# Last stage of a GNN + LSTM kernel: scale and shift of z2 moved into TensorE's products

## The reference

```
agg = A_hat @ x1                                  # per graph
h   = relu(batchnorm(agg @ W1.T + b1, g1, be1))   # 256 features
z2  = h @ W2.T + b2                               # 128 features
y   = (z2 - mean(z2)) * rsqrt(var(z2) + eps) * g2 + be2   # mean, var over all 16384 rows
out = layernorm(x1 + y)                           # over the 128 features of each row
```

## Time and profile before

| | us |
|---|---|
| median of 3 runs | 802.19 (801.57 to 805.52) |
| profiled execution, its own time | 802.61 |
| its span, first to last instruction | 800.8 |
| TensorE busy | 775.7 (97%) |
| VectorE busy | 716.3 (89%) |
| ScalarE busy | 596.7 (75%) |
| GpSimd busy | 107.7 (13%) |
| mean granted TensorE clock | 0.994 |

### The profile page before, as it was taken

One profiled execution on the slowest core, in us unless ns is written; L12 is line 12 of the kernel. 1 busy time (PEld: TensorE's weight loads), 2 busy tenths in 40 slices (PEclk: granted clock), 3 DMA queues, 4 the chain that ended last, 5 costly groups with the idle time before them and its releaser, 6 DMA issues.

```text
span 800.8 us, 15544 instructions
## 1 busy us (share of the span) xinstructions
PE 775.7 (97%) x4964; PEld 532.6 (67%) x4964; DVE 716.3 (89%) x1826; ACT 596.7 (75%) x1186; POOL 107.7 (13%) x117
## 2 busy tenths in 40 slices
PE   8999999999999999999999999999999989999995
PEld 6666777777767777777677767767776656444542
DVE  4787989999999999999999999999999988788996
ACT  4876777777777777777777778686868765697598
POOL 0000000000000000000000000000000101187695
PEclk9999999999999999999999999999999999999998
DMA  5010001010101010101010101010000000155245
GB/s 202 29 51 1 1 28 54 27 53 28 53 28 54 26 52 26 52 26 52 26 52 26 52 26 52 27 52 28 27 27 28 27 27 27 52 168 174 84 180 210
DMA packets 17694, 44.45 MB, mean 56 GB/s; under 512 B 2032, under 2 KB 3184, under 8 KB 17520
## 3 DMA queue, kind: packets, MB, share of 16 engines
q1 hardware_dynamic: 17504, 43.81, 15.2%
q10 hardware_dynamic: 144, 0.07, 0.0%
HBM read 27.09 MB, written 16.78 MB: 55 GB/s over the span
## 4 chain that ended last, share of the span: by engine, by line
PE 81%; DVE 9%; ACT 5%; issue 2%; DMA 1%; POOL 0%; ACTq 0%; DVEq 0%; POOLq 0%
PE gate_bank L964 15%; PE gate_bank L965 14%; PE gate_bank L979 6%; PE gate_bank L989 6%; PE gate_bank L1038 5%; PE front_bank L874 3%; PE back_bank L918 3%; ACT z L1187 3%; PE front_bank L879 3%; PE front_bank L891 3%; PE front_bank L885 3%; PE gate_bank L948 3%; PE gate_bank L949 3%; PE gate_bank L950 3%; PE gate_bank L972 3%
## 5 line engine op out<-in xcount | busy, mean ns | idle before, releaser
L964 PE MATMUL gate_bank<-h_hi,w_hi 128*128 128x256 f16 (+2 forms) x528 | 162.6, 308 | 4.4 <-DVE h_lo L1404 2.9
L965 PE MATMUL gate_bank<-h_hi,w_lo 128*128 128x256 f16 (+2 forms) x528 | 162.5, 308 | 0.0
L1126 ACT ACTIVATE gate_i<-gate_bank,lstm_bias 128x512 f32<-128x512 f32 (+2 forms) x176 | 99.5, 566 | 61.9 <-PE gate_bank L989 32.1
L1126 ACT ACTIVATE gate_o<-gate_bank,lstm_bias 128x512 f32<-128x512 f32 (+2 forms) x176 | 100.0, 568 | 31.2 <-PE gate_bank L989 20.8
L979 PE MATMUL gate_bank<-h_lo,w_hi 128*128 128x256 f16 (+2 forms) x384 | 116.1, 302 | 0.0
L964 PE MATMUL gate_bank<-s_hi,w_hi 128*128 128x256 f16 (+2 forms) x384 | 112.7, 302 | 0.6 <-DVE s_hi L1401 0.4
L1387 DVE SCALAR_TENSOR_TENSOR gate_f<-gate_o,gate_f 128x512 f32<-128x512 f32 (+2 forms) x176 | 94.7, 538 | 20.4 <-ACT gate_f L1132 19.4
L965 PE MATMUL gate_bank<-s_hi,w_lo 128*128 128x256 f16 (+2 forms) x384 | 112.6, 301 | 0.0
L765 POOL TENSOR_TENSOR rstd<-veps,neg_half 128x8 f32<-128x8 f32 x15 | 26.3, 1751 | 628.0 <-DVE veps L1326 628.0
L1132 ACT ACTIVATE gate_f<-cell 128x512 f32<-128x512 f32 (+2 forms) x176 | 89.7, 510 | 28.0 <-DVE cell L1384 14.7
L1126 ACT ACTIVATE gate_g<-gate_bank,lstm_bias 128x512 f32<-128x512 f32 (+2 forms) x176 | 99.5, 565 | 0.8 <-PE gate_bank L972 0.2
(11 more groups left out here) (261 smaller groups left out, 1722.2 us busy)
## 6 DMA issues: line engine op xcount, KB each, us to landing
x_kept<-normed_sb SPq DMA_DIRECT2D x16, 512.0 KB, 2.6
z<-x_kept SPq DMA_DIRECT2D x16, 512.0 KB, 3.7
rows_sb<-in_x SPq DMA_DIRECT2D x15, 512.0 KB, 3.3
x_front<-in_x SPq DMA_DIRECT2D x15, 512.0 KB, 4.5
out<-z SPq DMA_DIRECT2D x15, 512.0 KB, 3.1
z<-in_wr SPq DMA_DIRECT2D x1, 1536.0 KB, 7.0
x_front<-in_x SPq DMA_DIRECT2D x2, 256.0 KB, 3.7
out<-z SPq DMA_DIRECT2D x2, 256.0 KB, 2.6
```

What stands on the lines that cost most here:

```text
L964: mm(dst, w[0], v[0], start=start, stop=False)
L965: mm(dst, w[1], v[0], start=False, stop=False)
L1126: ins = activation(acts[gate][h][:, 0:n], gate_bank[h][bank_of(job, gate)][:, 0:n], ACT.Tanh if gate == "g" else ACT.Sigmoid, bias=lstm_bi ...
```

## The change

The step 1 above goes away, with its staging tile and `y_scaled`. The scale and the shift become two 128x128 tiles, `scale_diag` and `shift_diag`: the identity times the scale, and times the shift, made once by VectorE when the two are known. A third tile holds ones. All three lie in h0T. For each block of 128 columns TensorE now takes an ordinary fp32 product of z2 (stationary) with `scale_diag` (moving), which transposes and scales, and another of ones (stationary) with `shift_diag` (moving), which puts the shift into every row (`shift_in`). `x1_rows` is issued first, as the product that starts the bank. VectorE makes the ones at the start of the z2 stage, ahead of the splitting of W2. TensorE's loop over t is written out, with constant addresses.

```diff
@@ -477,7 +477,8 @@
         normed = normed_sb
-        scaled = [mixed, h0T, x_front, rows_sb]
+        scale_diag, shift_diag, ones = (h0T[:, 0, n * P:(n + 1) * P] for n in range(3))
         shapes = (("bn", (GB, 6)), ("comb", (3, GB)), ("veps", (GB,)), ("rstd", (GB,)), ("mean_rstd", (GB,)))
         terms = {name: [sb(name, [P, *shape])[:]] for name, shape in shapes}
...
@@ -637,20 +638,11 @@
         r_parts = [t[:].bitcast(F16) for t in (x_front, mixed, rows_sb)]
         z2_bank = [gate_bank[0][0], gate_bank[1][0], gate_bank[0][2], gate_bank[1][2]]
         LAST = HALVES // 4 - 1
-        free_at_start = [z2_kept, y_full, y_norm]
+        free_at_start = [z2_kept, y_norm]
         FIRST_LOADS, LOADS = 4, 8
         STAY_WARM = 20
         WARM_UP = 8
         block = ctx.enter_context(nc.Block())
-        def scale_z2(eng, n, t, u):
-            eng.wait_ge(y_full[u], 2 * t + 1)
-            eng.tensor_scalar(scaled[u][:, n, :],
-                              z[:, bass.ds(8 * t + (2 * u + n), 1), 0, :].rearrange("p o n -> p (o n)"),
-                              small[:, 1:2], small[:, 2:3], ALU.mult, ALU.add).then_inc(y_scaled[n][u], 1)
         def flat(t):
             return t.rearrange("p a n -> p (a n)")
...
@@ -788,9 +780,6 @@
                                                 parts[:, j, 0:BANK], ALU.subtract).then_inc(r_split, 1)
             pool.wait_ge(sem_bn2, 2)
             nc.gpsimd.tensor_tensor(small[:, 13:14], small[:, 12:13], neg_half[:, 0:1], ALU.pow).then_inc(sem_bn2_pow, 1)
-            pool.wait_ge(sem_bn2, 3)
-            for u in range(4):
-                scale_z2(pool, 1, 0, u)
             def row_powers(t, u, at=slice(0, GB), seen=0):
...
@@ -802,18 +791,12 @@
                 nc.gpsimd.tensor_tensor(mean_rstd[u][:, at], comb[u][:, 2, at], rstd[u][:, at], ALU.mult
                                         ).then_inc(y_shift[u], 1)
-            for u in range(4):
-                if u == 0:
-                    row_powers(0, 0, slice(0, 4))
-                    row_powers(0, 0, slice(4, 8), 1)
-                else:
-                    row_powers(0, u)
-                scale_z2(pool, 1, 1, u)
+            row_powers(0, 0, slice(0, 4))
+            row_powers(0, 0, slice(4, 8), 1)
+            for u in range(1, 4):
+                row_powers(0, u)
             for t in range(1, LAST + 1):
                 for u in range(4):
-                    if t < LAST:
-                        pool.wait_ge(y_mom[u], 4 * (t + 1 + (u == 0)))
-                        scale_z2(pool, 1, t + 1, u)
                     row_powers(t, u)
...
@@ -1049,21 +1032,28 @@
                           z[:, bass.ds(8 * t + (2 * u + n), 1), 1, :].rearrange("p o n -> p (o n)"),
                           start=first, stop=not first, skip_group_check=True)
+            def shift_in(to, stop=False):
+                for b in range(4):
+                    last = mm(to[:, b * P:(b + 1) * P], ones, shift_diag, start=False, stop=stop and b == 3,
+                              skip_group_check=True)
+                return last
+            def z2_rows(t, u, n, b, stop):
+                at = slice(b * P, (b + 1) * P)
+                return mm(row_bank[u][n][:, at],
+                          z[:, 8 * t + 2 * u + n, 0, at], scale_diag,
+                          start=False, stop=stop, skip_group_check=True)
             def rows_out(t, u, x1_there=()):
                 pe.wait_ge(y_norm[u], t + 1)
                 for n in range(2):
-                    to = row_bank[u][n]
-                    pe.wait_ge(y_scaled[n][u], t + 1)
+                    if n not in x1_there:
+                        x1_rows(t, u, n, True)
+                    shift_in(row_bank[u][n])
                     for b in range(4):
-                        at = slice(b * P, (b + 1) * P)
-                        if n in x1_there:
-                            last = mm(to[:, at], scaled[u][:, n, at], ident[:], start=False, stop=(b == 3),
-                                      skip_group_check=True)
-                        else:
-                            mm(to[:, at], scaled[u][:, n, at], ident[:],
-                               start=(b == 0), stop=False, is_transpose=True, skip_group_check=True)
-                    if n not in x1_there:
-                        last = x1_rows(t, u, n, False)
+                        last = z2_rows(t, u, n, b, b == 3)
                     last.then_inc(y_full[u], 1)
...
@@ -1074,10 +1064,20 @@
                 x1_rows(0, u, n, True)
             for m in range(2, 4):
                 pe.wait_ge(z2_kept[m], CHUNKS // 4 + 1)
-            for u in range(4):
-                rows_out(0, u, ((0, 1), (0,), (), ())[u])
+            pe.wait_ge(z2_terms, 2)
+            for b in range(4):
+                z2_rows(0, 0, 0, b, False)
+            pe.wait_ge(z2_terms, 3)
+            for n in range(2):
+                if n:
+                    for b in range(4):
+                        z2_rows(0, 0, n, b, False)
+                shift_in(row_bank[0][n], True).then_inc(y_full[0], 1)
+            rows_out(0, 1, (0,))
+            for u in range(2, 4):
+                rows_out(0, u)
             pe.wait_ge(x1_back_end, 32)
-            with pe.Fori(1, HALVES // 4) as t:
+            for t in range(1, HALVES // 4):
                 for u in range(4):
                     rows_out(t, u)
...
@@ -1180,24 +1180,17 @@
             with act.Fori(1, CHUNKS // TURN) as c:
                 relus(c)
-            def normed_rows(t, u, sets=range(2)):
-                for n in sets:
-                    for b in range(4):
-                        at = z[:, bass.ds(8 * t + (2 * u + n), 1), 1, b * P:(b + 1) * P]
-                        ins = activation(at.rearrange("p o n -> p (o n)"), row_bank[u][n][:, b * P:(b + 1) * P],
-                                         ACT.Identity, bias=mean_rstd[u][:, 4 * n + b:4 * n + b + 1],
-                                         scale=rstd[u][:, 4 * n + b:4 * n + b + 1])
+            def normed_rows(t, u, first=0, count=GB):
+                for k in range(first, first + count):
+                    n, b = k // 4, k % 4
+                    at = z[:, bass.ds(8 * t + (2 * u + n), 1), 1, b * P:(b + 1) * P]
+                    ins = activation(at.rearrange("p o n -> p (o n)"), row_bank[u][n][:, b * P:(b + 1) * P],
+                                     ACT.Identity, bias=mean_rstd[u][:, k:k + 1], scale=rstd[u][:, k:k + 1])
                 return ins
-            act.wait_ge(sem_bn2, 3)
-            for t, u in ((0, 1), (0, 2), (0, 3), (1, 0)):
-                act.wait_ge(y_full[u], 2 * t + 1)
-                activation(scaled[u][:, 0, :], z[:, 8 * t + 2 * u, 0, :], ACT.Identity, bias=small[:, 2:3],
-                           scale=small[:, 1:2]).then_inc(y_scaled[0][u], 1)
             for n in range(2):
                 act.wait_ge(y_shift[0], n + 1)
-                ins = normed_rows(0, 0, (n,))
+                ins = normed_rows(0, 0, 4 * n, 4)
             ins.then_inc(y_norm[0], 1)
             for u in range(1, 4):
                 act.wait_ge(y_shift[u], 1)
...
@@ -1463,6 +1456,7 @@
             last.then_inc(sem_bn1, 1)
+            ve.memset(ones, 1.0).then_inc(z2_terms, 1)
             ve.tensor_scalar(gw2_sb[:], gw2_sb[:], W_SCALE, None, ALU.mult).then_inc(w2_ready, 1)
             dve.wait_ge(w2_ready, 1)
             ve.tensor_copy(w2_hi, gw2_sb[:]).then_inc(w2_ready, 1)
...
@@ -1544,31 +1538,32 @@
                 return ve.scalar_tensor_tensor(out=veps_t, in0=m2, scalar=1.0 / P, in1=veps_t, op0=ALU.mult,
                                                op1=ALU.add)
-            def row_terms(t, u, scaled_next, sets=range(2), seen=0):
+            def row_terms(t, u, sets=range(2), seen=0, between=()):
                 first_twice = 1 if u == 0 and not seen and not (isinstance(t, int) and t == 0) else 0
                 at = slice(4 * sets[0], 4 * sets[-1] + 4)
                 for n in sets:
-                    dve.wait_ge(y_full[u], 2 * t + n + 2)
+                    dve.wait_ge(y_full[u], 2 * t + n + 1)
                     last = row_stats(row_bank[u][n], bn[u], n)
                 last.then_inc(y_mom[u], 1)
                 for step in range(3):
                     dve.wait_ge(y_mom[u], 4 * (t + first_twice + seen) + step + 1)
                     row_steps(bn[u][:, at, :], comb[u][:, :, at], veps[u][:, at], step).then_inc(y_mom[u], 1)
-                    if step == 1 and scaled_next:
-                        scale_z2(dve, 0, *scaled_next)
+                    if between:
+                        between[step]()
             dve.wait_ge(sem_bn2, 3)
-            scale_z2(dve, 0, 0, 0)
-            row_terms(0, 0, None, (0,))
-            row_terms(0, 0, None, (1,), 1)
+            for k, to in enumerate((scale_diag, shift_diag)):
+                ve.tensor_scalar(to, ident[:], small[:, 1 + k:2 + k], None, ALU.mult).then_inc(z2_terms, 1)
+            row_terms(0, 0, (0,))
```

(11 more changed lines are left out.)

## The result

The changed kernel takes 838.8 us (median of 4 runs, 837.5 to 839.51) against 802.24 before: a ratio of 1.0451, 95% interval 1.0439 to 1.0464. It was run again beside the later experiments and gave 838.05 us, 1.0449 (1.0435 to 1.0463). The profiled execution took 838.18 us with a span of 836.4, so 1.8 us lie around the span as before. The prediction was 839.8, with a span of 838.0.

What follows compares the result with a forecast made beforehand. TensorE, with next to no slack in the last stage, was taken as the bound: start 746.10 + ones 0.2 + products 82.5 + last record 0.16 + tail 9.0 = 838.0 us span, 1.8 around it, 839.8 us; range 835.5 to 845.

Steps and rivals of the forecast that it cites:

- The pitch: Last stage, TensorE: each added full fp32 product of 128 columns takes 0.225 us, 256 of them 57.6 us.
- The ones: Start of the z2 stage: VectorE's memset ahead of splitting W2 delays TensorE by 0.2 us, bounds 0 and 0.3.
- The two tiles, and the first product: Last stage's start: scale's tile takes VectorE 0.34 us, TensorE starts 0.14 later; shift's tile is hidden by the first products.
- No waits on the other engines: Last stage: the others need near half of TensorE's 5.3 us step, so TensorE runs without a gap.
- The 4.9 us of waiting: Last stage before: TensorE's waiting and restarting within 45.3 us, already contained in the subtraction; relieving other engines gives nothing beyond.
- The tail: After TensorE's last product: the same chain to the end as before, 9.0 us; stores possibly 0.7 sooner, not counted.
- B: Last stage: weight loads and products take turns, 0.30 us a record, 154 us in place of 57.6; 936 us, chance 0.02.
- C: Last stage: new products cost 0.11 us each like a transpose, 28.2 us in all; 810.4 us, chance 0.02.
- D: TensorE's steady set: added products fit into what the bound leaves, not slower, down to about 800 us; chance 0.02.
- E: Written-out loop over t: straight code starves TensorE, 0.3 us a set, adding 7 us; 847 us, chance 0.04.

Runs made afterwards that it cites:

- the runs with the dead scalings: Changed kernel with the old 512-column scalings still made on VectorE and GpSimd into unread tiles: 840.85 us; without those of the last turn, 838.4 us.
- the run with the shift's products alone: Kernel before, engines still scaling z2, but the shift comes from 128 products of ones with its diagonal: 825.89 us.
- the wide product with a quarter of the loads: Changed kernel with each set's shift as one fp32 product of 512 columns in place of four of 128: 836.98 us.
- the addition: Changed kernel, but VectorE and GpSimd add the shift to x1 in SBUF before its product: 817.76 us; with GpSimd's addition under VectorE's statistics, 812.39 us.

## Why the prediction was right

The step and its mechanism were as forecast: 839.8 us against a median of 838.8, and against 838.18 for the profiled execution, whose terms follow, in us:

| term | predicted | measured |
|---|---|---|
| VectorE begins the scale's tile | 745.62 + 0.2 | 745.25 |
| from there to TensorE's first product | 0.48 | 0.44 |
| first to last product | 82.66 | 827.99 − 745.69 = 82.30 |
| tail | 9.0 | 836.4 − 827.99 = 8.4 |
| span | 838.0 | 836.4 |

The terms are off by 0.6, 0.04, 0.4 and 0.6 us, all in the same direction, so no error hid another. The two largest lie outside TensorE's stage.

**The pitch** was read from L1060's products, which stood in the kernel before only because three sets had x1 ahead of time. Taken at 0.225, measured 0.223 to 0.224: 0.4 us of the sum.

**The ones** were priced at 0.2 us on TensorE's path and cost 0.01 there. Around them, after:

```profile
690.28 0.34 DVE L1453 SCALAR_TENSOR_TENSOR small<-small,v_sb 128x1 f32<-128x1 f32 x2
690.60 0.17 DVE L1459 MEMSET h0T<- 128x128 f32 x1
690.68 0.23 DVE L1460 TENSOR_SCALAR gw_sb<-gw_sb 128x256 f32<-128x256 f32 x1
```

The next operation begins 0.08 us after the memset, but VectorE does pay: counted from the start of the operation ahead (690.66 before, 690.28 after), the splitting ends after 1.32 us before and 1.42 after. TensorE's first product of the z2 stage comes 1.56 and 1.57 us after the same point, because it had something else ahead of it, 20 warm-up products, here before:

```profile
687.90 4.48 PE L837 MATMUL gate_bank<-s_hi 128*128 128x512 f16 x20
```

They take 20 × 0.216 us, to 692.22, exactly where that first product starts, and after the change from 687.53 to 691.85, the same. VectorE's result was there 0.24 us ahead of it before and is 0.15 us ahead now. So the prediction's reading, that TensorE waits for VectorE's result here, was wrong: there was at least 0.1 us of slack, and the memset fell into it. The other 0.4 us by which the stage begins early were there before this point, in code that the change doesn't touch; the second profile of the same kernel begins the tile at 744.62, so this part of the sum is chance.

**The two tiles, and the first product,** came within 0.04 us, with the row of L1332 as the measure; the tile's own operation takes 0.28 us where 0.34 was taken, and TensorE starts 0.16 after it.

**No waits on the other engines** held: there is no wait of TensorE for ACT, and the runs with the dead scalings show the relief of VectorE and GpSimd worth nothing. **The 4.9 us of waiting**, which only the subtraction has in it, showed in the run with the shift's products alone.

**The tail** was put at 9.0 and is 8.4. The prediction said that none of its engines is late for another reason, and that ACT's backlog ends where the last four start; but 791.26 + 4.61 = 795.87 lies 0.37 us past that start. Two things differ. ACT's last four took 1.76 us from first start to last end behind that backlog, some 0.71 each, and take 1.50, some 0.46 each, when ACT comes to them idle:

```profile
831.72 1.50 ACT L1187 ACTIVATE z<-front_bank,gate_i 128x128 f32<-128x128 f32 x4 [3.79 <-POOL gate_i L791]
...
833.24 0.83 SPq L737 DMA_DIRECT2D out<-z  x2
```

And from the issue of the last stores to the end there are 836.4 − 833.24 = 3.2 us where there were 3.5. The store ahead of them was issued 1.34 us earlier before and 2.25 us earlier after, and DMA is busy for 0.37 of the tail after where it was for 0.62; that earlier transfers held up the last ones is inferred from this, no run takes them apart. Together the two are the 0.6 us; the prediction had allowed up to 0.7 for the stores and counted nothing. The other profiles agree: the tail is 9.0 us in the two kernels with the backlog (before, and before written out), and 8.4 in all that end with an idle ACT, the kernel before with the shift's products among them; only the dead scaling at the end makes it 8.76.

**The rivals.** B (loads bare, 936) is excluded by the result; the wide product with a quarter of the loads shows that they cost next to nothing at 128 columns. C and D (810 and about 800) fell with the pitch: a full product never came under two records' worth. E (the straight code, 847) was tried apart and is nothing, and the changed kernel's stage has no gap.

## What to carry to other kernels

Work that other engines do beside the bound was free here, put back or taken away, as long as it didn't push another engine over the bound, as the addition did; moved onto the bound it costs its full pitch, and "let the matmul do it" is a real price where a transpose of one record at 0.11 us becomes a full fp32 product of two at 0.22, with a second for a constant that only has to be added. Look for the new operation in the old trace before costing it: a corner case had it here, and the sum came within 1.6 us of a span of 836. Subtract from TensorE's sum not the old busy time but the old stretch, waits and all, since the waits go as the engine fills. To test such a sum, compare the stage in the profiles, where four experiments met their forecast differences within 0.05 us, and not only the whole time, whose runs spread by 1 to 3 us.

## What the runs showed of the hardware that was not expected

An operation of VectorE on 128x8 that takes 0.16 us took 1.24 when GpSimd had begun to add two tensors of 128x512 just before it, to the end of that addition; the reverse, GpSimd held by VectorE's addition, 0.46 in place of 0.20. VectorE's statistics (one input, in PSUM) weren't touched. GpSimd's old scaling, with one input of 128x512, holds VectorE up in the same way; the trace of the kernel before shows it twice, at 748.40 and at 752.69 (0.50 us), each time to the end of the scaling:

```profile
748.20 0.76 POOL L650 TENSOR_SCALAR rows_sb<-z,small 128x512 f32<-128x512 f32 x1
...
748.40 0.58 DVE L1537 SCALAR_TENSOR_TENSOR comb<-bn 128x4 f32<-128x4 f32 x1
```

In the steady steps of the run with the dead scalings it lay beside VectorE's waiting and held nothing up. GpSimd's power on 128x8, 1.64 us or more, holds up none of VectorE's small operations: they take 0.16 to 0.17 us under it, before and in the later runs. And in the kernel before with the shift's products, where the scaling takes 1.57 us, an L1545 that begins 0.3 us into it is held (0.39 us), to 0.7 us after the scaling's start, while one that begins 1.2 us into it is not (0.17). So it is not the whole instruction that shuts VectorE out; which part of it does isn't shown. Moving one instruction in GpSimd's order was worth 5.4 us.
